# Selective scans: the skip term by products with diagonals, and some C products on VectorE

## The reference, cut to what matters

```
def step(h, inp):                       # first layer; the second has the same form
    dA_t, dBx_t, C_t = inp              # dA = exp(delta*A), dBx = delta*u*B
    h = dA_t * h + dBx_t
    y = einsum('bdn,bn->bd', h, C_t)    # sum over the 16 states
    return h, y
y = ys + D * x                          # the skip term
```

## Time and profile before

| | before |
|---|---|
| median of 3 runs | 3770.78 us |
| the profiled execution | 3770.48 us |
| its span | 3768.8 us |
| granted TensorE clock, mean | 0.965 of full speed |
| busy over the span | TensorE 94%, VectorE 59%, ScalarE 40%, GpSimd 35% |
| `BS`, first VectorE instruction to last | 1081.0 to 1245.8 us |
| `ES0` | 3283.5 to 3453.5 us |
| `ES1` | 3478.4 to 3648.2 us |

### The profile page before, as it was taken

The page is one execution under the profiler, slowest core; times in us unless marked ns, Lnnn a source line. Parts: engine busy times, 40 slices in busy tenths (PEclk is TensorE's granted clock), DMA queues, the critical chain, the costliest instruction groups (busy, mean ns, idle before and its releaser), DMA issues. The chain is left out here.

```text
span 3768.8 us, 78281 instructions
## 1 busy us (share of the span) xinstructions
PE 3526.6 (94%) x34520; PEld 2686.0 (71%) x34520; DVE 2236.8 (59%) x2305; ACT 1525.5 (40%) x2169; POOL 1324.6 (35%) x652
## 2 busy tenths in 40 slices
PE   7999999999779689999999999999999998797998
PEld 4566666665369556888888888888888846597974
DVE  4677777777269832555555555555555515597962
ACT  2555555555279311222222222222222102587850
POOL 3344444442079321112222222222221004396961
PEclk9999999999789889999999999999999998898999
DMA  6455555553111042111111111111111212011110
GB/s 206 129 148 151 147 148 153 150 142 91 40 62 57 4 162 82 34 43 39 41 35 42 50 42 51 42 50 42 51 42 46 74 43 56 35 54 37 51 48 23
DMA packets 215257, 277.27 MB, mean 74 GB/s; under 512 B 67056, under 2 KB 165328, under 8 KB 213632
## 3 DMA queue, kind: packets, MB, share of 16 engines
q1 hardware_dynamic: 214920, 272.28, 24.5%
HBM read 218.63 MB, written 53.13 MB: 72 GB/s over the span
## 5 line engine op out<-in xcount | busy, mean ns | idle before, releaser
L1780 POOL TENSOR_TENSOR D_ctx_lo<-D_ctx_raw,D_ctx_hi 128x2048 fp32r<-128x2048 f32 (+1 forms) x64 | 269.5, 4212 | 1204.4 <-ACT D_ctx_hi L1774 1204.4
L740 DVE TENSOR_REDUCE A_mxc<-A_psX 128x2 f32<-128x768 f32 (+2 forms) x512 | 480.8, 984 | 117.0 <-PE A_psX L782 113.1
L1057 ACT ACTIVATE A_probs<-A_psE 128x1024 f32<-128x1024 f32 (+1 forms) x416 | 426.3, 1025 | 292.7 <-PE A_psE L1115 290.5
L1799 ACT ACTIVATE D_V<-D_psY 128x384 f32<-128x384 f32 x208 | 101.9, 490 | 890.6 <-PE D_psY L1865 890.6
L1815 DVE TENSOR_REDUCE D_mxc<-D_psE 128x4 f32<-128x1536 f32 (+2 forms) x128 | 241.9, 1890 | 204.2 <-PE D_psE L1893 204.2
L2156 ACT ACTIVATE D_probs<-D_psE 128x2048 f32<-128x2048 f32 x112 | 210.5, 1879 | 295.9 <-PE D_psE L2269 295.9
L2285 PE MATMUL D_psO<-D_probs,D_V 128*32 128x256 f32 (+1 forms) x5376 | 313.3, 381 | 0.0
L335 DVE TENSOR_TENSOR_SCAN E_du<-ES_dA,ES_dB 128x1024 f32<-128x1024 f32 x128 | 288.4, 2281 | 20.5 <-PE ES_dB L373 13.2
L1865 PE MATMUL D_psY<-D_wv_hi,D_ctx_hi 128*128 128x384 f32 x832 | 285.7, 343 | 0.0
L1855 PE MATMUL D_psY<-D_ctx_hi,D_wk_hi 128*128 128x384 f32 (+2 forms) x768 | 279.8, 364 | 0.5 <-POOL D_ctx_lo L1780 0.5
L1865 PE MATMUL D_psY<-D_wv_hi,D_ctx_lo 128*128 128x384 f32 x832 | 279.1, 336 | 0.0
(11 more groups left out here) (380 smaller groups left out, 7948.2 us busy)
## 6 DMA issues: line engine op xcount, KB each, us to landing
A_land<-in_ctx SPq DMA_DIRECT2D x32, 768.0 KB, 5.6
D_ctx_raw<-in_ctx SPq DMA_DIRECT2D x32, 768.0 KB, 4.6
A_land<-in_ctx SPq DMA_DIRECT2D x16, 1024.0 KB, 5.9
D_ctx_raw<-in_ctx SPq DMA_DIRECT2D x16, 1024.0 KB, 5.8
E_Cn<-bc_scratch SPq DMA_DIRECT2D x64, 256.0 KB, 3.2
k_scratch<-A_Khl SPq DMA_DIRECT2D x32, 384.0 KB, 4.1
A_Kst<-k_scratch SPq DMA_DIRECT2D x64, 192.0 KB, 3.6
A_land<-in_ctx SPq DMA_DIRECT2D x16, 642.0 KB, 4.2
```

The costliest lines, as they stand in the source:

```text
L740: nc.vector.tensor_reduce(mxc[:, u % 4, :, u // 4], psX[:, x % 2, :, 0:w], axis=AX_X, op=ALU.max).then_inc(x_free, 1)
L1057: nc.scalar.activation(probs[0:KW[k], n % NPR, :, :].rearrange("p h q -> p (h q)"), psE[0:KW[k], :], ACT.Exp, scale=HD ** -0.5).then_inc(e ...
L1780: nc.gpsimd.tensor_tensor(ctx_lo[c][:, :, 0:w], ctx_raw[c][:, :, 0:w], ctx_hi[c][:, :, 0:w].bitcast(F32), ALU.subtract).then_inc(lo_done[c ...
```

## The change

Three things in `scan_states`; nothing else is touched.

1. The skip term. GpSimd makes four 128x128 diagonals (identity times D, `skip_diag`) in place of four 128x1024 products. In `add` the 8 extra transposes of a last step become 8 real fp32 products of the raw tile with `skip_diag`.
2. C products. In steps 5, 13, 21, ... 61 (`s % 8 == 5`, in every fourth state) the product of the second chunk (128x512) is made by VectorE right after its scan, and GpSimd makes only the first chunk's. The last step's product is VectorE's alone, in two instructions. The semaphore `hc_ready` becomes `hc_pool` and `hc_dve`.
3. `scaled` holds only the two full tiles, the diagonals get a tile of their own (`b_diag`). `entering` runs tile by tile, and in steps 0 and 1 it waits for each tile alone. Its instructions are the same in kind and number.

```diff
-        scaled = r.sb("scaled", [P, NS, TILES, CN * P])
+        SCALED = 2
+        scaled = r.sb("scaled", [P, NS, SCALED, CN * P])
+        b_diag = r.sb("b_diag", [P, NS, TILES - SCALED, P])
+        skip_diag = r.sb("skip_diag", [P, CN, P])
...
+        def product_on_dve(s, j):
+            return s == len(STEPS) - 1 or (s % 8 == 5 and j == 1)
...
             def _(pool):
                 for c in range(CN):
-                    nc.gpsimd.tensor_scalar(skip[:, c, :], skip[:, c, :], skip_col(c), None, ALU.mult
+                    nc.gpsimd.tensor_scalar(skip_diag[:, c, :], consts["ident"][:, :], skip_col(c), None, ALU.mult
                                             ).then_inc(skip_ready, 1)
...
+                    mine = [j for j in range(W) if not product_on_dve(s, j)]
+                    if not mine:
+                        continue
...
-                    nc.gpsimd.tensor_tensor(hc[s % NP][:, :, :], h[:, s % NH],
-                                            rows.C[:, q % NR, :].unsqueeze(1).broadcast_to([P, W, HALF]), ALU.mult
-                                            ).then_inc(hc_ready, 1)
+                    of = slice(mine[0], mine[-1] + 1)
+                    nc.gpsimd.tensor_tensor(hc[s % NP][:, of, :], h[:, s % NH, of, :],
+                                            rows.C[:, q % NR, :].unsqueeze(1).broadcast_to([P, len(mine), HALF]), ALU.mult
+                                            ).then_inc(hc_pool, 1)
...
                     if s >= NH:
-                        dve.wait_ge(hc_ready, s - NH + 1)
+                        dve.wait_ge(hc_pool, pool_products(s - NH))
...
+                def product(s, j):
+                    q = ring_q(*STEPS[s][0:2])
+                    dve.wait_ge(h_ready, s + 1)
+                    dve.wait_ge(summed, s - NP + 1)
+                    dve.wait_ge(rows.c_in[q % NR], 16 * (q // NR + 1))
+                    nc.vector.tensor_tensor(hc[s % NP][:, j, :], h[:, s % NH, j, :], rows.C[:, q % NR, :], ALU.mult
+                                            ).then_inc(hc_dve, 1)
...
                 for s in range(len(STEPS)):
                     scan(s)
+                    for j in range(W):
+                        if product_on_dve(s, j):
+                            product(s, j)
                     if s - 3 in nth_last:
                         finish(s - 3)
...
-                    pe.wait_ge(scaled_ready, TILES * (m + 1))
                     if s >= NE:
+                        pe.wait_ge(scaled_ready, TILES * (m + 1))
                         pe.wait_ge(h_ready, s - NE + 1)
-                    for j, c in enumerate(chunks(s)):
-                        for i in range(TILES):
+                    for i in range(TILES):
+                        if s < NE:
+                            pe.wait_ge(scaled_ready, TILES * m + i + 1)
+                        for j, c in enumerate(chunks(s)):
...
+                        for i in range(TILES):
+                            last = nc.tensor.matmul(acc[:, c, bass.ts(i, P)], hc[s % NP][:, j, bass.ts(i, P)],
+                                                    consts["ident"][:, :], start=(n == 0 and i == 0), stop=False,
+                                                    is_transpose=True, skip_group_check=True)
                         if n == N_STATE - 1:
                             pe.wait_ge(skip_ready, CN)
-                            parts.append(tokens(skip, c, half))
...
+                                last = nc.tensor.matmul(acc[:, c, bass.ts(i, P)], tokens(skip, c, half)[:, bass.ts(i, P)],
+                                                        skip_diag[:, c, :], start=False, stop=True, skip_group_check=True)
```

More of the change, by code:

```diff
@@ L236, in scan_states @@
         scaled_ready, db_full = r.sem("scaled_ready"), r.sem("db_full")
-        h_ready, hc_ready, summed = r.sem("h_ready"), r.sem("hc_ready"), r.sem("summed")
+        h_ready, summed = r.sem("h_ready"), r.sem("summed")
+        hc_pool, hc_dve = r.sem("hc_pool"), r.sem("hc_dve")
         copied, turned, finished = r.sem("copied"), r.sem("turned"), r.sem("finished")
@@ L255, in piece, with dve_products, pool_products @@
             if diagonal(i):
-                return scaled[:, m % NS, i, 0:P], consts["ident"][:, :], b_col(t, m % N_STATE)
+                return b_diag[:, m % NS, i - SCALED, :], consts["ident"][:, :], b_col(t, m % N_STATE)
             return scaled[:, m % NS, i, :], duT[:, t, :], b_col(t, m % N_STATE)
         def diagonal(i):
-            return i >= TILES - 2
+            return i >= SCALED
+        def product_on_dve(s, j):
+            return s == len(STEPS) - 1 or (s % 8 == 5 and j == 1)
+        def dve_products(s):
+            return sum(1 for k in range(s + 1) for j in range(W) if product_on_dve(k, j))
+        def pool_products(s):
+            return sum(1 for k in range(s + 1) if not all(product_on_dve(k, j) for j in range(W)))
         with nc.Block() as block:
@@ L268, in _ @@
                     if q < rows.total:
-                        sp.wait_ge(hc_ready, CP * (k + 1))
+                        sp.wait_ge(hc_pool, pool_products(CP * (k + 1) - 1))
+                        if dve_products(CP * (k + 1) - 1):
+                            sp.wait_ge(hc_dve, dve_products(CP * (k + 1) - 1))
                         rows.load_c(sp, q)
@@ L365, in entering @@
                     m = N_STATE * half + n
-                    pe.wait_ge(scaled_ready, TILES * (m + 1))
                     if s >= NE:
+                        pe.wait_ge(scaled_ready, TILES * (m + 1))
                         pe.wait_ge(h_ready, s - NE + 1)
-                    for j, c in enumerate(chunks(s)):
-                        for i in range(TILES):
+                    for i in range(TILES):
+                        if s < NE:
+                            pe.wait_ge(scaled_ready, TILES * m + i + 1)
+                        for j, c in enumerate(chunks(s)):
                             to = dB[:, s % NE, j, bass.ts(i, P)]
                             if diagonal(i):
-                                last = nc.tensor.matmul(to, duT[:, TILES * half + i, bass.ts(c, P)], scaled[:, m % NS, i, 0:P],
-                                                        start=True, stop=True)
+                                last = nc.tensor.matmul(to, duT[:, TILES * half + i, bass.ts(c, P)],
+                                                        b_diag[:, m % NS, i - SCALED, :], start=True, stop=True)
                             else:
@@ L381, in add @@
                     half, n, cp = STEPS[s]
-                    pe.wait_ge(hc_ready, s + 1)
+                    if pool_products(s):
+                        pe.wait_ge(hc_pool, pool_products(s))
+                    if any(product_on_dve(s, j) for j in range(W)):
+                        pe.wait_ge(hc_dve, dve_products(s))
                     if half and n == 0:
```

6 lines of the change are left out of this document (removed).

## The result

The changed kernel takes 3791.01 us (median of 4 runs, 3788.81 to 3794.98) beside 3771.59 us for the kernel before (3769.69 to 3772.8) on the same chip: a ratio of 1.0053, with a 95% interval from 1.0042 to 1.0065. It is slower, as forecast, but by 19.4 us (half a per cent) where 11.8 us were forecast. The profiled execution took 3790.59 us, its span is 3788.9 (before 3768.8). Two executions far outside the others of their kernel, one of 5756 us (one scan later) and one of 3959 us (the kernel before), are left out of the ratios.

What follows compares the result with a forecast made beforehand. GpSimd was taken to bound the scan loop at 2.33 us a step, three engines right behind. Start, loop, middle and tail gave +3.9 us in BS and +3.95 twice in ES: +11.8 on 3770.5, 3782 us, range 3765 to 3796.

Steps and rivals of the forecast that it cites:

- likeliest case: Whole kernel: blocking of VectorE's products by GpSimd as worked out, 3776 to 3788 us, chance 0.56.
- Start: Start of each region: narrow diagonals and earlier TensorE work end scan 4 sooner, -3.7 us in BS, -3.9 in ES.
- T(4): End of scan 4 counted from the region's memset: 16.0 to 16.1 us, before 19.8 in BS and 19.9 in ES1.
- The scans at 2.177 us: Loop, steps 5 to 63: 59 scans at VectorE's own pace cost 128.4 us.
- The rival of a falling clock in the loops: TensorE's clock falls in half of the 24 product places, and at the tails: 3797 us, chance 0.12.
- Blocking: Loop: VectorE's product, both inputs in SBUF, waits for GpSimd's running product and ends 0.54 us after it.
- The price of a product: Loop: delay of the next scan by a VectorE product, 1.76 us; in all 13.3 us in BS, 12.6 in ES.
- 0.76 + L: Loop: delay per VectorE product; L, 0.99 us, is how long after scan s-1 ends GpSimd starts product s-1.
- T(63): End of the last scan counted from the region's memset: 161.0 us in BS (157.0 before), 164.0 in ES (159.9).
- The middle: From the end of scan 31 to that of scan 36: skip products and finish add 3.2 us in BS, 6.9 in ES.
- The tail: After the last scan: -0.65 us by an earlier end, +0.5 us (0 to 1.7) for TensorE's slow clock.
- no blocking: VectorE's products do not wait for GpSimd's and cost 0.97 us each: 3767 us, chance 0.20.

Runs made afterwards that it cites:

- one scan later: Changed kernel, but VectorE issues the product of step s behind scan s+1: 3765.54 us, ratio 0.9986 to the kernel before.
- one-input kernel: Changed kernel with VectorE's 24 loop products replaced by a maximum of h over the same 128x512 elements: 3776.97 us, ratio 1.0009.
- the filler: Changed kernel plus twenty identity transposes into an unused dB buffer in TensorE's idle time before the last two additions: 3786.4 us, ratio 1.0034.
- products alone: Changed kernel with the skip term as before (wide products on GpSimd, transposes on TensorE), VectorE's products kept: 3800.06 us, ratio 1.0066.
- diagonals alone: Changed kernel with all C products back on GpSimd, skip diagonals and new tile order kept: 3770.52 us, ratio 0.9989.
- skip products in the loop: Changed kernel with TensorE's skip products moved behind the additions of steps 12, 20, 44 and 52: 3774.89 us, ratio 1.0014.
- the kernel without VectorE's products: Changed kernel with skip products behind the additions of steps 12, 20, 44 and 52 and all C products on GpSimd: 3764.03 us, ratio 0.9985.

## Why the prediction was right in its direction and too low in its size

The sum was +11.8 us; the regions measured +23.8, and the whole kernel +19.4. Its 3791 us lie inside the range of the prediction, but above the 3776 to 3788 of its likeliest case. By the steps of the prediction:

- **Start, right.** T(4) was to be 16.0 to 16.1 us; it is 16.03 in BS and 16.04 in ES0. A diagonal costs 0.6 us, not 0.4, which nothing waits for.
- **The scans at 2.177 us, right**, and the clock in the loop stays at 1.00 through the idle time of some 1.7 us that a product leaves TensorE. The rival of a falling clock in the loops is out.
- **Blocking, right as a mechanism.** VectorE's product was to end about 0.5 us behind GpSimd's; it ends 0.55 behind, in all 24 places. The one-input kernel and the one-scan-later kernel show it, and that a GpSimd instruction that is already queued doesn't get in first twice.
- **The price of a product, too small: 1.76 us forecast, 2.05 measured** (the first 1.0 and 1.26, the one behind the middle 1.7 and 1.97 in BS, 1.05 and 1.27 in ES). The formula 0.76 + L holds; the size of L failed. I had GpSimd start level after each product and L = 0.99. In the trace scan s-1 ends at 1115.56 and its product starts at 1116.85: L = 1.29. Most of the missing 0.3 is the wait of 0.23 us at 1105.18. GpSimd's product of step s+2 takes the `hc` buffer of step s. The addition of step s stands on TensorE behind the entering of step s+3, and that waits for scan s+1, which VectorE's product has made late. I followed that queue for VectorE's wait, and not for GpSimd's next one. T(63) is therefore 163.42 us in BS (161.0 forecast) and 166.45 in ES0 (164.0): 2.4 us a region, 7.2 in all.
- **The middle, right.** T(36) - T(31) is 14.25 us in BS and 17.85 in ES0; 14.1 and 17.8 were forecast.
- **The tail, too short.** I took 0.5 us for the slow clock, from 0 to 1.7. It costs 1.6 us in BS and ES0 and 2.7 in ES1, as the filler shows. I had worked out an idle time of 2.3 us and had a row with a fall after 2.5 us, so the upper end was the nearer one, and that I should have taken. In ES1 even that is too little, because the lower clock lasted 6.8 us there, longer than the some 3 us of that row. Some of this is chance: after the same idle time the clock did not fall in BS of the kernel with the products alone, so the true term was between 0 and 2.7 us a tail. The tails are 1.2, 1.2 and 2.3 us longer than forecast, 4.8 in all.

The two sizes make 12.0 us, the difference between 11.8 and 23.8. The 3.7 us that the same code lost elsewhere hides part of it in the span. The end above, no blocking at 3767 us, would have been nearly right for a kernel that issues the product one scan later (3765.5), but for another reason: there the blocking is still present, only short.

## What to carry to other kernels

When work moves from the engine that bounds to the one behind it, ask where in the partner's instruction it will be issued: the same product costs 2.05 us in most of its places right behind its scan and 0.96 one scan later. Two things set that, an addition that the product waits for and the instruction with two SBUF inputs that GpSimd is in the middle of. And compare with a kernel in which nothing is moved: at 0.96 us the products still made the loops no shorter than with the diagonals alone, and the gain lay in the tails. And look at what the moved work leaves idle at the end of a stage: additions that follow an idle time of TensorE may run at half rate (in eight of nine tails after 2.40 us here), so move what doesn't depend on the last result out of them.

## What the runs showed of the hardware

- A 128x512 product of VectorE with both inputs in SBUF takes 0.67 us alone. Issued while GpSimd's product is under way it takes 0.75 to 1.56 us, by how long that still runs, and ends 0.55 us after it: in all 24 places of the changed kernel. A 128x512 maximum with one input takes 0.69 us beside the same GpSimd instruction, and the scan of 128x1024, one input in SBUF and one in PSUM, 2.18 us from start to start beside it.
- It costs GpSimd too: the half product takes 1.73 us when VectorE's is under way at its start and 1.27 when VectorE scans.
- After an idle time of TensorE of 2.39 to 2.40 us in a tail the granted clock fell to 0.50 in eight of nine places (changed kernel, products alone, skip products in the loop) and stayed at 1.00 in one. After 2.13 to 2.15 us it fell in one of three (one input). It stayed at 1.00 through idle times of 1.06 us in tails and of up to 1.67 in the loops. But short idle times are not safe: in the kernel without VectorE's products it fell in BS's tail after three of 1.09, 1.21 and 1.22 us with 8 transposes between each two, and not in the tails of ES0 and ES1 after the same.
- Twenty transposes in the idle time, with no other product, kept it at 1.00 in three tails.
- How long the lower clock lasted differed between tails of the same program: 3.4 us in BS and ES0 and 6.8 in ES1, after idle times of 2.40, 2.40 and 2.39 us. What decides that, and whether it falls, stays open.
